# A hybrid block's attention stage: q, k, v and z projections by Strassen's seven half products, z by way of DRAM, and the inverse's evictions on ScalarE

## The reference

```
xn = layernorm(x)
mixed = silu(conv4(xn @ w_qkv));  q, k, v = split(mixed)   # w_qkv: 512 x 8192
z = xn @ w_z                                               # w_z: 512 x 4096
q, k = l2norm(q) * 128**-0.5, l2norm(k)                    # two value heads share one key head
beta, g = sigmoid(xn @ w_b), -exp(A_log) * softplus(xn @ w_a + dt_bias)
for each token: state *= exp(g); delta = (v - k state) * beta; state += k^T delta; o = q state
o = norm_w * rmsnorm(o) * silu(z)
x = x + o @ w_out
```

## Time and profile before

| | |
|---|---|
| median of 3 runs (lowest to highest) | 4213.05 us (4209.45 to 4213.18) |
| span of the profiled execution | 4212.1 us |
| TensorE / VectorE / ScalarE / GpSimd busy over the span | 98% / 81% / 55% / 11% |
| attention stage | start to about 3005 us |
| HBM traffic, mean | 61 GB/s |

### The profile page before, as it was taken

The page is one execution under the profiler, slowest core; times in us unless marked ns, Lnnn a source line. Parts: engine busy times, 40 slices in busy tenths (PEclk is TensorE's granted clock), DMA queues, the critical chain, the costliest instruction groups (busy, mean ns, idle before and its releaser), DMA issues. The chain is left out here.

```text
span 4212.1 us, 83193 instructions
## 1 busy us (share of the span) xinstructions
PE 4121.2 (98%) x30843; PEld 2520.6 (60%) x30843; DVE 3409.2 (81%) x8712; ACT 2324.0 (55%) x5479; POOL 461.8 (11%) x470
## 2 busy tenths in 40 slices
PE   8999999999999999999999999998899999999999
PEld 4566666666666666666666666666544444444444
DVE  5888888888888888888888888888546989898940
ACT  4555555555555555555555555555445656564643
POOL 1111111211111211111211111111000000000000
PEclk9999999999999999999999999999999999999999
DMA  2111111111111102201111111100103545454510
GB/s 77 43 34 36 39 34 41 34 32 39 39 32 44 34 32 79 66 32 44 34 31 39 39 32 44 34 29 22 67 1 115 164 148 168 149 173 154 182 60 10
DMA packets 202469, 263.52 MB, mean 63 GB/s; under 512 B 18222, under 2 KB 101426, under 8 KB 202066
## 3 DMA queue, kind: packets, MB, share of 16 engines
q1 hardware_dynamic: 202066, 258.20, 19.4%
HBM read 249.24 MB, written 8.91 MB: 61 GB/s over the span
## 5 line engine op out<-in xcount | busy, mean ns | idle before, releaser
L546 PE MATMUL bank<-x_blocks,w_qkv 128*128 128x512 f32 x2048 | 925.4, 595 | 4.9 <-ACT raw L831 4.2
L546 PEld LDWEIGHTS bank<-x_blocks,w_qkv 128*128 128x128 f32 x2048 | 374.4, 192 | 393.2 <-issue 374.5
L1169 DVE SCALAR_TENSOR_TENSOR conv<-raw,conv_w,conv 128x1024 f32<-128x1024 f32 x384 | 516.2, 1344 | 66.7 <-ACT conv L805 57.4
L663 PE MATMUL bank<-w_out_unit,oT 128*128 128x512 f32 x1008 | 487.6, 606 | 0.3 <-ACT oT L857 0.3
L498 PE MATMUL bank<-w_z_unit,x_blocks 128*128 128x256 f32 x2048 | 487.4, 379 | 0.0
L498 PEld LDWEIGHTS bank<-w_z_unit,x_blocks 128*128 128x128 f32 x2048 | 368.2, 190 | 40.4 <-issue 0.7
L831 ACT COPY raw<-bank 128x512 f32<-128x512 f32 x256 | 149.0, 582 | 324.4 <-PE bank L546 324.4
L1443 PE MATMUL bank<-xnT_f,w_gu 128*128 128x512 f32 x704 | 325.2, 606 | 1.2 <-ACT xnT_f L1942 0.9
L1462 PE MATMUL bank<-w_down,hidden 128*128 128x512 f32 x704 | 316.8, 593 | 1.7 <-DVE x_blocks L1521 1.7
L1452 PE MATMUL bank<-xnT_f,w_gu 128*128 128x512 f32 x704 | 316.8, 593 | 0.5 <-DVE hidden L1483 0.5
L2012 ACT ACTIVATE step_decay<-dt,rate 128x512 f32<-128x512 f32 x256 | 183.4, 720 | 216.5 <-DVE h L2121 214.2
(11 more groups left out here) (254 smaller groups left out, 7832.5 us busy)
## 6 DMA issues: line engine op xcount, KB each, us to landing
rows_b<-bc_rows SPq DMA_DIRECT2D x256, 256.0 KB, 3.4
rows_c<-bc_rows SPq DMA_DIRECT2D x256, 256.0 KB, 3.6
w_qkv<-in_w_qkv SPq DMA_DIRECT2D x128, 256.0 KB, 2.9
decay<-gc_rows SPq DMA_DIRECT2D x64, 512.0 KB, 4.0
w_z_unit<-in_w_z SPq DMA_DIRECT2D x32, 512.0 KB, 4.6
w_out_unit<-in_w_out SPq DMA_DIRECT2D x32, 512.0 KB, 5.1
x_after<-x SPq DMA_DIRECT2D x16, 256.0 KB, 2.0
x_blocks<-x_after SPq DMA_DIRECT2D x4, 1024.0 KB, 11.3
```

Of the source, the lines that this page charges most:

```text
L546: made = e.matmul(PROJ[:, :], w_qkv[:, p % 2, j, :], xnT[:, n // HK, j, h * BANK:(h + 1) * BANK], start=j == 0, stop=j == KT - 1)
L663: made = e.matmul(out_rows(N, t)[:, :], turned_to(N, t)[:, r, :], w_out[:, N % 2, r, :], start=r == 0, stop=r == REP - 1)
L1169: e.scalar_tensor_tensor(acc, raw[:, i % 2, tap:tap + T], conv_w[:, tap, col:col + 1], acc, ALU.mult, ALU.add).then_inc(on["conv"], 1)
```

## The change

A pair of weight tiles (K with Q, V0 with V1, or the two z tiles) makes a 2 by 2 block product: two column tiles times two token halves, over two halves of the inner dimension. Before, it took eight block products; now seven. The seven products of a pair run in the order 1, 2, 5, 4, 3, 7, 6, alternately in banks PROJ and ZB, and from the fourth on each adds onto what its bank holds. A product is two matmuls of 512 columns. The sums of x that Strassen needs are made once per batch by VectorE (`part_sums`) and held in SBUF; those of the second batch go through DRAM. The sums of weights are made by GpSimd for every pair. The 21 products of a unit are spread over its slots 0 to 7 as 2, 3, 2, 3, 3, 2, 3, 3, at three places "a", "b", "c" of the slot (with two, at "a" and "c"). ScalarE reads steps 0, 3 and 4 of each pair, VectorE steps 1, 2, 5 and 6.

z is now made with q, k and v, with channels on the partitions; it goes to DRAM by four stores per unit and comes back by two loads, in slots 19 and 23. `o` is no longer multiplied by z before it is turned; the eviction of the turned `o` multiplies by z and norm_w on VectorE (`gate_out`). The transposes of `o` on TensorE stand right behind the state products. The inverse's evictions, but for one addition and the turns, are on ScalarE. On VectorE `gate_out` stands behind `resid`, read "a" ahead of the convolution, read "b" behind the inverse's section 1, and read "c" behind `o` and ahead of the sections 0, 2 and 3. u is stored with its sign turned, which saves `neg_e_gc`.

```diff
@@ constants
-INVERSE, SCAN, ZPROJ, WOUT = 13, 16, 17, 23
+INVERSE, SCAN, WOUT = 13, 16, 23
-INV_STEPS = 12
+INV_STEPS, INV_COPIES = 4, 5
+ORDER = (1, 2, 5, 4, 3, 7, 6)
+UNIT_PRODUCTS = PAIRS * PRODUCTS
+ACT_STEPS, DVE_STEPS = (0, 3, 4), (1, 2, 5, 6)
+def products_of(slot):
+    unit, k = divmod(slot, PER_UNIT)
+    first, last = (UNIT_PRODUCTS * (k + i) // PER_UNIT for i in range(2))
+    made = [UNIT_PRODUCTS * unit + at for at in range(first, last)]
+    return dict(zip("abc" if len(made) == 3 else "ac", made))
...
+            else:
+                tile = 4 * unit + 2 * q + (1 if step in (3, 6) else 0)
+                before = {0: tile - 1, 1: tile - 3, 2: tile - 1, 3: tile - 3}[tile % 4]
+                if before >= 0:
+                    e.wait_ge(on["conv"], 3 * before + 3)
@@ sync
+                    if N is not None:
+                        e.wait_ge(on["z_store0"], 32 * (N + 1))
...
+                        rows = dram["z"][N].rearrange("(r p) t -> p r t", p=P)[:, :, a * BANK:(a + 1) * BANK]
+                        e.dma_start(z[:, :, a * BANK:(a + 1) * BANK], rows).then_inc(on[f"z_load{a}"], 16)
@@ tensor
+            def product(g):
+                pair, step = pair_step(g)
+                unit, q = divmod(pair, PAIRS)
+                m, bank = ORDER[step], product_bank(g)
+                if g >= 2:
+                    if pair_step(g - 2)[1] in ACT_STEPS:
+                        e.wait_ge(on["act_read"], act_count(g - 2))
+                    else:
+                        e.wait_ge(on["dve_read"], dve_count(g - 2))
...
+                for j in range(2):
+                    made = e.matmul(bank[:, :], weight[:, j, :], part(0, m)[:, j, :], start=j == 0 and step < 3, stop=j == 1,
+                                    skip_group_check=True)
+                made.then_inc(on["product"], 1)
@@ tensor, in the slot: behind the state products
-                    for j in range(KT):
-                        made = e.matmul(PROJ[:, :], w_qkv[:, p % 2, j, :], xnT[:, n // HK, j, h * BANK:(h + 1) * BANK],
-                                        start=j == 0, stop=j == KT - 1)
-                    made.then_inc(on["proj"], 1)
+                n_out, t_out = unit_at(slot, WOUT)
+                if n_out is not None:
+                    N, t = n_out, t_out
+                    for ahead in turned_in(N, t):
+                        at = 8 * N + ahead
...
+                        if N < UNITS - 1:
+                            if at > 0:
+                                e.wait_ge(on["x_add"], at)
...
+                        for r in range(REP):
+                            made = e.transpose(turned_o(N, ahead)[:, r, :], o[:, at % O_RING, r, :], c["ident"][:, :])
+                        made.then_inc(on["oT_pe"], 1)
+
+                if "a" in products:
+                    product(products["a"])
...
-                gates(slot, 0, split)
+                if "b" in products:
+                    product(products["b"])
@@ tensor, before the state update
+                if "c" in products:
+                    product(products["c"])
@@ scalar
+                read_at(slot, "a")
...
-                        e.wait_ge(on["raw"], 2 * p + 2)
+                        done = PRODUCTS * (PAIRS * N + i // 2) + 5 + i % 2
+                        e.wait_ge(on["dve_read"], dve_count(done))
+                        e.wait_ge(on["act_read"], act_count(done))
...
-                    e.copy(raw[:, i % 2, PAD + h * BANK:PAD + (h + 1) * BANK], PROJ[:, :]).then_inc(on["raw"], 1)
+                read_at(slot, "b")
...
-                    e.copy(u[:, :, :], two(UB, 0)).then_inc(on["u_copy"], 1)
+                    e.mul(u[:, :, :], two(UB, 0), 1.0 if t_scan == 0 else -1.0).then_inc(on["u_copy"], 1)
@@ vector
+            def read_product(g):
...
+                if step in (1, 2):
+                    e.tensor_tensor(total, bank, total, ALU.add).then_inc(on["dve_read"], 1)
+                else:
+                    wait_result_free(e, unit, q, step)
+                    e.tensor_tensor(result_place(q, step), bank, total, ALU.subtract).then_inc(on["dve_read"], 1)
+            def gate_out(slot):
...
+                        e.scalar_tensor_tensor(turned_to(n, ahead)[:, :, :], turned_o(n, ahead), norm_w[:, 0:1],
+                                               z[:, :, ahead * P:(ahead + 1) * P], ALU.mult, ALU.mult).then_inc(
+                            on["oT_copy"], 1)
...
+                gate_out(slot)
...
+                read_at(slot, "a")
...
+                read_at(slot, "b")
...
+                read_at(slot, "c")
@@ gpsimd
+                for g in products_of(slot - 1).values():
+                    pair, step = pair_step(g)
+                    if pair + 1 < PAIRS * UNITS and step in (2, 6):
+                        weight_sums(pair + 1, (1, 2) if step == 2 else (5, 6))
```

More of the change, by code:

```diff
@@ L130, with product_slot, pair_step, act_count @@
 BASE_STEPS = 4 + 4 + 3 * (BASE - 2) + 1
-INV_STEPS = 12
+INV_STEPS, INV_COPIES = 4, 5
 K, Q, V0, V1 = range(4)
+KQ_PAIR, V_PAIR, Z_PAIR = range(3)
+PAIRS = 3
+ORDER = (1, 2, 5, 4, 3, 7, 6)
+PRODUCTS = len(ORDER)
+UNIT_PRODUCTS = PAIRS * PRODUCTS
+ACT_STEPS, DVE_STEPS = (0, 3, 4), (1, 2, 5, 6)
+PARTS = 7
+PLACE = {(0, 0): 2, (1, 1): 5, (0, 1): 3, (1, 0): 4}
+SUMS_AT = {1: 0, 2: 1, 5: 2, 7: 3, 6: 4}
+SUM_COUNT = {1: 1, 2: 1, 5: 2, 7: 3, 6: 4}
+Z_STAGE = {3: 0, 4: 1, 5: 2, 6: 0}
+def product_slot(g):
+    unit, at = divmod(g, UNIT_PRODUCTS)
+    return PER_UNIT * unit + next(k for k in range(PER_UNIT) if at < UNIT_PRODUCTS * (k + 1) // PER_UNIT)
+def products_of(slot):
+    if not 0 <= slot < PER_UNIT * UNITS:
+        return {}
+    unit, k = divmod(slot, PER_UNIT)
+    first, last = (UNIT_PRODUCTS * (k + i) // PER_UNIT for i in range(2))
+    made = [UNIT_PRODUCTS * unit + at for at in range(first, last)]
+    return dict(zip("abc" if len(made) == 3 else "ac", made))
+def pair_step(g):
+    return divmod(g, PRODUCTS)
+def act_count(g):
+    pair, step = pair_step(g)
+    return len(ACT_STEPS) * pair + sum(s <= step for s in ACT_STEPS)
+def dve_count(g):
+    pair, step = pair_step(g)
+    return len(DVE_STEPS) * pair + sum(s <= step for s in DVE_STEPS)
 def unit_at(slot, first):
@@ L304, in sync @@
                         e.wait_ge(on["gc_store"], 32 * (b + 1))
-                n, k = unit_at(slot, 0)
-                if n is not None and k % 2 == 1 and 4 * n + k // 2 + 2 < 4 * UNITS:
-                    e.wait_ge(on["proj"], 8 * n + k + 1)
-                    load_part(4 * n + k // 2 + 2)
+                if slot == 9:
+                    e.wait_ge(on["part_sum"], 10)
+                    for m in range(1, PARTS + 1):
+                        e.dma_start(dram["x_parts"][m - 1].rearrange("p (k t) -> p k t", k=2), part(1, m)).then_inc(
+                            on["part_store"], 16)
@@ new lines, in sync @@
+                for g in products_of(slot - 1).values():
+                    pair, step = pair_step(g)
+                    if step == 4 and pair + 2 < PAIRS * UNITS:
+                        e.wait_ge(on["product"], g + 1)
+                        e.wait_ge(on["w_sum"], 4 * (pair + 1))
+                        load_pair(pair + 2)
+                for g in products_of(slot - 1).values():
+                    pair, step = pair_step(g)
+                    if pair == PAIRS * HK - 1:
+                        m = ORDER[step]
+                        e.wait_ge(on["product"], g + 1)
+                        e.wait_ge(on["part_store"], 16 * PARTS)
+                        if step >= 2:
+                            e.wait_ge(on[f"part_load{step % 2}"], 16 * (step // 2))
+                        e.dma_start(halves[:, m - 1, :, :], dram["x_parts"][m - 1].rearrange("p (k t) -> p k t", k=2)).then_inc(
+                            on[f"part_load{step % 2}"], 16)
@@ L510, in tensor @@
             turn_rows(0, range(NC))
-            e.wait_ge(on["xnT"], NC)
+            gate_sums(0)
             for slot in range(ATTENTION_SLOTS):
+                products = products_of(slot)
                 n_scan, t_scan = unit_at(slot, SCAN)
@@ L730, in evict_rows, with read_at @@
                     e.wait_ge(on["xn_turned"], NC * b + t + 1)
-                    e.copy(xnT[:, b, :, t * P:(t + 1) * P],
-                           (QB, OB)[t % 2][:, :].rearrange("p (j w) -> p j w", w=P)).then_inc(on["xnT"], 1)
+                    e.copy(turned_tiles(b, t), (QB, OB)[t % 2][:, :].rearrange("p (a k w) -> p a k w", a=2, k=2)).then_inc(
+                        on["xnT"], 1)
+            def read_product(g):
+                pair, step = pair_step(g)
+                unit, q = divmod(pair, PAIRS)
+                e.wait_ge(on["product"], g + 1)
+                if step == 0:
+                    if pair >= 2:
+                        e.wait_ge(on["dve_read"], len(DVE_STEPS) * (pair - 1))
+                    e.mul(common[:, pair % 2, :], product_bank(g)[:, :], -1.0).then_inc(on["act_read"], 1)
+                else:
```

(6 more changed lines are left out.)

443 lines of the change are left out of this document (241 added, 202 removed).

## The result

The changed kernel takes 4795.7 us (median of 4 runs, 4789.7 to 4804.8) against 4211.5 of the kernel before on the same chip: ratio 1.139, 95% interval 1.137 to 1.141, 14% slower. The forecast was 4640 us with a range to 4790. The sign and the chain through the slots held; the time is 156 us above the forecast and just above the range, because the price of TensorE's low clock was set far too low. It is also nearly the value of the third rival (4790), which is partly luck, as told further down.

A forecast was written before the change was run, and what follows sets the result against it. TensorE bounds the kernel, VectorE close behind; the change chains each slot through the wait on x_add. 102.4 us a unit plus two additions gives +14.1 over 29 units (409 us); 4212.1 + 409 + 20 for the head: 4640 us, range 4390 to 4790.

The forecast's parts named there:

- the chain through the slots: Attention slots, one x_add's end to the next: dependent pieces add up to 102.4 us a unit against 90.6.
- TensorE's low clock: Phase 1, after 4.3 us idle in phase 0: clock falls once, costing 1.7 us a unit, bounds 0 and 6.8.
- the third rival: TensorE in the attention units: clock falls after each long wait, 5.1 us more a unit, 4790 us; chance 0.14.
- both additions: On top of the slots' 102.4 us a unit: 0.7 for GpSimd's weight sums and 1.7 for TensorE's low clock.
- VectorE's added work: VectorE per unit: product reads 7.2 us and gatings 3.4 added, gate multiplies and inverse evictions 8.8 removed, net +1.8.
- The first rival: Transposes' wait on x_add is covered, TensorE stays the bound: about 4060 us, faster; chance 0.10.
- the second (only the end of the slot bites): Only the wait before the transposes bites, TensorE sets mid-slot: +5.6 us a unit, 4395 us; chance 0.16.
- GpSimd's sums: GpSimd's 12 weight sums a unit slow VectorE, one beside phase 2's conv: 0.7 us a unit, bounds 0 and 3.5.
- Head: Slots before the attention stage: 18 us more TensorE work, 6 for sums of x, 4 given back; 20 us.
- The tail: Slots from 256 on: z gone (up to 29 us), same coupling added in like amount; 0, ±20 us.
- The clean-up and z through DRAM: z stores and loads and inverse evictions on ScalarE: nothing, up to a few us a unit if loads are late.

The follow-up runs named there:

- both additions removed: Changed kernel with matmuls filling TensorE's idle stretches and GpSimd's sums of weights made for the first pair only: 4611.8 us, 102.90 us a unit.
- the tap's experiment: Changed kernel with ScalarE's tap ahead of read "a": 4609.4 us, 102.92 us a unit.
- the orders put right: Changed kernel, transposes back behind u, gating ahead of conv (phases 0, 2), tap ahead of read "a", read "b" behind u copy: 4342.3 us; with second-batch x sums later, 4337.4.
- the filled run with the orders and the head put right: Changed kernel with transposes, gating, ScalarE's reads and second-batch x sums reordered, plus unread matmuls in TensorE's waits of phases 1 and 5: 4326.6 us.
- u first: Changed kernel with ScalarE's read "b" behind its copy of u: 4790.1 us.
- no sums: Changed kernel with transposes, gating, ScalarE's reads and second-batch x sums reordered, and GpSimd's weight sums for the first pair only, unfilled: 4378.2 us.

## What of the prediction was right, and the step that failed

**The chain: right.** TensorE's largest wait is the one before the transposes, then phase 4's for u; ScalarE waits for conv once a unit; phase 5 is the shortest slot and phase 4 the longest. With both additions removed each slot is where the sum put it (102.7 us at the full clock for 102.4). VectorE's added work was costed at 1.8 us a unit and is 1.7 without the sums (79.0 us against 77.3). Its busy share came to 0.74, not "near 0.8", and TensorE's to 0.88 for "about 0.85". The first rival (TensorE stays the bound) and the second (only the end of the slot bites) were rightly put behind it: by the tap's experiment the middle of the slot counts.

**TensorE's clock: the step that failed.** The forecast gave the low clock 1.7 us a unit: one fall, behind phase 0's idle time of 4.3 us ("Phase 0 leaves TensorE idle 4.3 us before phase 1 ... 1.7 us"), and it wrote off the waits of 2.3 to 2.9 us as a bound. Measured at 103.6 us a unit for the full clock, it costs 5.6, which is 3.9 too little, 29 × 3.9 = 113 us. The fall that was counted is there, behind a wait of 4.16, but it costs 2.7 us: in phase 1 the clock is low for 6.3 us in the mean and not for 3.3. The falls that were left out, behind waits of 2.25, 2.99 and 2.76 us, cost the rest, 1.7 of it in phase 3. The low stretches of the unit shown lose about 7 us of TensorE's time (busy time times one minus the granted clock, summed over the 2 us windows); 5.6 of them are in its length, the rest lay under VectorE's work.

The third rival put 5.1 us more on the clock, 6.8 in all, and was nearest, at a chance of 0.14. That its time of 4790 is within 6 us of the measured one is luck: it has 35 us too much for the clock and 41 too little for the rest. Its own sign, a clock row below 0.85, was not met (0.92 in the unit). What the Trainium skill, "TensorE: Matmul & The Clock Gate", section "HAM oscillation — how this bites in real kernels", says, that waits between bursts bring the low clock back each time, agrees with this trace only in part: behind the waits of 4.16, 2.99 and 2.76 us in every unit, behind the one of 2.25 in 13 of 27, and never behind those of 1.4 us and less.

**GpSimd's sums: nearly right.** Taken at 0.7 us a unit, they cost 0.9 at the full clock. Taking them away from the changed kernel gave 2.4, but 1.5 of that went with falls of the clock. The forecast had no term for this coupling: with other work beside VectorE the clock falls in another number of units. Here taking the sums away made the falls fewer; with the orders put right it made them more, at equal waits, and why stays open.

**Head: 48 us, forecast 20.** Slot 6's conv starts at 73.2 us in the changed kernel and at 60.6 before: the slots there are a chain of product, read, tap and conv as later, which I had costed as TensorE time only. The place of the second batch's sums of x is 5 us of the rest. The tail was right: 0 forecast, −4.

A unit came out 4.5 us longer than forecast: 3.9 for the clock, 0.2 for the sums, 0.3 for the chain and 0.1 of rounding. In 29 units that is 131 us, with 28 of the head and −4 of the tail 155 of the 156 us.

**The clean-up and z through DRAM: nothing found.** No wait on a load or store of z is among the larger ones of TensorE, VectorE or ScalarE. No run took these parts away, so their price was not measured.

**What the change was worth at its best.** A product takes 1.75 us from start to start in the filled run with the orders and the head put right, as costed, so TensorE's work on products did fall by about 5 us a unit. Its whole busy time fell by less, from 90.4 to 87.8 us in the same kernel without filling; where the difference lies was not followed up. But VectorE got reads and gatings for it and has 80.7 us of work a unit, 77.3 before; the best unit is 93.5 us, 3 more than before. That VectorE's queue is what remains is read from the waits; it was not tested by taking work from VectorE.

## What to carry to other kernels

When a wait is moved ahead of the work that covered it, price the cover first: this one move cost 13.6 of the 18.6 us a unit by itself. When a forecast makes TensorE wait in every slot, put the low clock behind the longer waits into the sum, not into the range, and ask of each low stretch whether it lies in a slot that TensorE sets. When an experiment takes a term away, count the falls of the clock in both traces before the whole difference is put down to the term: here 1.5 of 2.4 us were the clock's. And read an experiment by phases: one that changes nothing in the total (u first) or goes the wrong way (no sums) can still have done what it should in its own phase.

## What the runs showed of the hardware

- The clock fell behind waits much shorter than those that I had counted: behind 2.25 us in the changed kernel, behind 1.65 us in the kernel before with the transposes moved, and in the version with the orders put right and without sums behind two of 0.89 and 0.66 us close together.
- Equal waits did not do the same each time: the wait of 2.25 us brought the low clock in 13 of 27 units, the one of 1.65 in 14, and one of 1.75 us in another phase of that kernel in none; the two of 0.89 and 0.66 in all units without the sums and in 1 of 27 with them. Which of the two happens can't be read from the waits alone, and was not settled.
- GpSimd's work on SBUF beside VectorE's three-operand conv made that slower. In the changed kernel 222 of its instructions had no GpSimd work beside them and took 1285 ns in the mean, 162 had some and took 1567. The mean over all was 1404 ns with the sums of weights and 1288 without; with the orders put right it was 1448 and 1345.
- Matmuls whose results are not used, put into TensorE's waits, made the changed kernel 130 us faster (4795.7 to 4665.9).
